# Two attention stages: loops unrolled, four slots of q and K, K loaded once per head group, value products two key tiles at a time

## The chip, the cores and the metric

The kernel runs on one core of a Trainium2 chip. Its engines are TensorE (PE; a weight load, PEld, goes ahead of each matmul), VectorE (DVE), ScalarE (ACT), GpSimd (POOL) and SyncE (SP), which issues the DMAs. Each runs its own list of instructions in order and waits on semaphores for the others. The metric is the time of one execution in microseconds (us), the median of several runs; lower is better.

## The reference

Four blocks on x (1024 tokens by 512), each followed by a residual sum and a layer norm: a causal self-attention with an adapter, a lookup block, a second causal self-attention, and a gated feed-forward block. The change touches the inside of the two attentions:

```python
# layer 0: 32 heads of 16 for q, k and v; layer 1: 32 heads of q, 8 of k and v (4 q heads share one)
scores = einsum("bhqd,bhkd->bhqk", q, k) / sqrt(16)      # q, k after rotary embedding
scores = where(causal, scores, -inf)
attn = softmax(scores, axis=-1)                          # T = 1024 tokens
y = einsum("bhqk,bhkd->bhqd", attn, v)
```

## The kernel before

An attention is done in 8 **head groups** g of R = 4 heads. A group has two **units**, c = 0 (queries 0 to 511, 4 key tiles of 128) and c = 1 (queries 512 to 1023, 8 key tiles), because of the causal mask. For each unit:

- **Maxima** (`entry`, L841 to L868). The row maxima of the scores are found ahead: PE multiplies a query tile (96 rows: q and k are cut into bf16 parts that are stacked) with `k_max` into one of three PSUM banks (`RING`), adds a mask on the diagonal (L866), and DVE takes the maximum into `mx` (L1035). One such piece is an *entry*: 12 entries for c0, 28 for c1. After the last one DVE joins the halves (L1042, c1 only) and cuts the maxima into three bf16 parts in four dependent operations on 16 columns (L1046 to L1053). One more entry, "T", is PE's transpose of these parts (L850); DVE copies it to `mT` (L1024), and SP copies `mT` in three DMAs (`load_max`, L805) into rows 96 to 98 of the stacked q. The maxima of group g+1 are done while group g is in its scores and values; entries are dealt out evenly over the *slots* between them (`slot`, L918).
- **Scores** (L883): `k_exp` (96 rows and 3 rows of -1) times the stacked q with its maxima, 99 rows deep, so that the product comes shifted by its maximum. Two heads are a *pair* n; pairs use two PSUM pairs in turn, so pair n waits for exp n-2 (L879).
- **Exp** (L980) on ACT, into one of `NP_RING` = 4 buffers of `arena_p`.
- **Masking** (L1098): POOL zeroes what lies above the diagonal in the last four key tiles of a unit with `affine_select`.
- **Values** (L903): four matmuls in float32 of 32 columns each, side by side in the array, per key tile; then ACT copies the sum to `o_raw` (L987). POOL copies the v of a group to `v_grp` (L1078).

In the loop (`step`, L923 to L937) each key tile has: scores of the next tile (pair, slot, pair, slot), slot, values of this tile, slot. Two groups are one turn of a hardware loop (`Fori`), so that DMA addresses come from registers.

SP loads from DRAM what `load_and_project` stored there: q of a unit (3 DMAs, 2 slots per c), and K of a group twice, as `k_max` and as `k_exp` (3 DMAs each, 2 slots each; the rows of one part are read for 3, 2 and 1 stacked parts: `broadcast_to`, L711). `k_max` of group g+2 is loaded into the slot of group g once the maxima of g+1 that stand ahead are done. SP's list is in order: `mT`, q, `k_exp`, `mT`, q, `k_max`. In layer 1 K has 1 head for a group, not 4. `load_first` is issued earlier, for layer 0 in the adapter stage, for layer 1 between the stores of the projection (L362).

Of the kernel before, what the change touches and what calls it, by code (L numbers as in the profile page):

```python
# [32 lines left out]
P = 128  # L33
# [5 lines left out]
R = 4  # L39
# [16 lines left out]
NP_RING = 4  # L56
# [49 lines left out]
def build(nc, d, out):  # L106
    with ExitStack() as stack:
# [13 lines left out]

        arena_s = at("arena_s", M_S, [P, 12288])
# [74 lines left out]
        attention(nc, 0, att, stacked, arena_o, arena_p, v_tok, v_grp, ident_b, maskb, psum)  # L197
# [15 lines left out]
        attention(nc, 1, att, stacked, arena_o, arena_p, v_tok, v_grp, ident_b, maskb, psum)  # L213
# [468 lines left out]
class StackedOperands:  # L682


    def __init__(self, ph, layer, arena_s, q_parts, k_parts):
        self.q_parts, self.k_parts = q_parts, k_parts
        self.kr = R if layer == 0 else 1
        self.q = view(arena_s, 0, [2, CH, R * 512], BF16)
        self.k_max = view(arena_s, 16384, [2, R * T], BF16)
        self.k_exp = view(arena_s, 32768, [2, R * T], BF16)  # L690
        self.q_loaded = [[ph.sem(f"q_loaded{s}{c}") for c in range(CH)] for s in range(2)]
        self.km_loaded = [ph.sem(f"km_loaded{s}") for s in range(2)]
        self.ke_loaded = [ph.sem(f"ke_loaded{s}") for s in range(2)]
# [6 lines left out]
    def load_q(self, sp, g, s, c):  # L700

        for j0, n in ((0, 3), (3, 2), (5, 1)):
            sp.dma_start(
                self.q[D * j0:D * (j0 + n), s, c, :].rearrange("p (h t) -> p h t", h=R),
                self.q_parts[bass.ds(R * g, R), 0:n, :, 512 * c:512 * c + 512]
                .rearrange("h j d t -> j d h t")).then_inc(self.q_loaded[s][c], 16)

    def load_k(self, sp, g, s, dst, sem):

        for kp, (j0, n) in enumerate(((0, 3), (3, 2), (5, 1))):  # L710
            sp.dma_start(  # L711
                dst[D * j0:D * (j0 + n), s, 0:self.kr * T],
                self.k_parts[kp, :, bass.ds(self.kr * g, self.kr), :]
                .rearrange("(o d) h t -> o d (h t)", o=1).broadcast_to([n, D, self.kr * T]))\
                .then_inc(sem[s], 16)

    def load_first(self, queue):

        self.load_q(queue, 0, 0, 0)
        self.load_k(queue, 0, 0, self.k_max, self.km_loaded)  # L720


def attention(nc, layer, phase, stacked, arena_o, arena_p, v_tok, v_grp, ident_b, maskb, psum):
# [4 lines left out]


    kr, q_st, k_max, k_exp = stacked.kr, stacked.q, stacked.k_max, stacked.k_exp  # L730
    q_loaded, km_loaded, ke_loaded = stacked.q_loaded, stacked.km_loaded, stacked.ke_loaded
# [1136 lines left out]
```

## Time and profile before

| | |
|---|---|
| time, median of 3 runs (lowest, highest) | 1092.92 us (1092.42 to 1098.62) |
| profiled execution: its span | 1084.4 us |
| what lies around the span (median less span) | 8.5 us |
| TensorE busy | 924.4 us, 85% |
| VectorE busy | 700.9 us, 65% |
| ScalarE busy | 485.7 us, 45% |
| GpSimd busy | 254.2 us, 23% |
| mean granted clock of TensorE | 0.917 |
| attention stages | about 150 to 471 us (layer 0) and 635 to 900 us (layer 1) |

Busy time is the sum over the instructions of an engine. The granted clock is the share of its full rate that TensorE was allowed; it is 1.0 (2.4 GHz) or 0.5 (1.2 GHz) at any one time. The span is from the first to the last instruction of the profiled execution.

### The profile page before, as it was taken

What the parts mean: (1) busy time and instruction counts of PE and PEld (TensorE: products, weight loads), DVE (VectorE), ACT (ScalarE), POOL (GpSimd) and SP (SyncE); (2) the same over time, 40 slices, a digit from 0 to 9 for tenths busy, and PEclk for the clock granted to TensorE, in tenths of its full rate; (3) what the DMA queues carried; (4) which work ended last, traced back from release to release, by engine and by line L of the source; (5) the groups of instructions that cost most, each with busy time, mean ns of one, the idle gap of its engine ahead of it and who ended that gap; (6) DMA issues with size and microseconds to landing.
All of it is one profiled execution on the core that took longest, in us unless ns stands there. A gap on an engine that the chain in (4) does not pass through costs nothing. (4 is left out here: it accounts for less than half of the span.)

```text
span 1084.4 us, 17334 instructions
## 1 busy us (share of the span) xinstructions
PE 924.4 (85%) x5462; PEld 512.0 (47%) x5462; DVE 700.9 (65%) x1305; ACT 485.7 (45%) x750; POOL 254.2 (23%) x397
## 2 busy tenths in 40 slices
PE   7879943789988898888977877999999988799998
PEld 5557821333333333257535532333444426677766
DVE  6975332668666766448584765988888835745564
ACT  4221401336544655642262213566666673346730
POOL 2554020022112111210614531221212223012300
PEclk9998965889889989999788977999999999999999
DMA  9221161112211321020001330011111101042001
GB/s 315 88 89 59 23 144 42 42 48 87 71 56 59 81 72 54 11 97 1 1 0 56 103 94 23 24 46 46 46 44 44 24 1 39 11 173 78 20 21 59
DMA packets 45537, 64.87 MB, mean 60 GB/s; under 512 B 9056, under 2 KB 32160, under 8 KB 43936
## 3 DMA queue, kind: packets, MB, share of 16 engines
q1 hardware_dynamic: 45472, 64.01, 19.7%
q8 instruction: 40, 0.66, 0.3%
q14 instruction: 25, 0.20, 0.1%
HBM read 51.27 MB, written 12.32 MB: 59 GB/s over the span
## 5 line engine op out<-in xcount | busy, mean ns | idle before, releaser
L1035 DVE TENSOR_REDUCE mx<-psum 128x1 f32<-128x512 f32 (+3 forms) x640 | 372.1, 632 | 157.9 <-PE psum L866 132.1
L980 ACT ACTIVATE arena_p<-psum 128x1024 f32<-128x1024 f32 (+3 forms) x384 | 294.0, 808 | 271.5 <-PE psum L883 270.7
L861 PE MATMUL psum<-arena_s 96*128 96x512 bf16 (+3 forms) x768 | 236.7, 349 | 53.8 <-DMA arena_s<-k_parts 43.4
L883 PE MATMUL psum<-arena_s 99*128 99x512 bf16 (+3 forms) x768 | 191.1, 340 | 30.3 <-DMA arena_s<-mT 26.7
L1098 POOL TENSOR_SCALAR_AFFINE_SELECT arena_p<-arena_p 128x256 f32<-128x256 f32 x256 | 102.8, 407 | 472.5 <-ACT arena_p L980 470.7
L903 PE MATMUL psum<-arena_p,v_grp 128*32 128x512 f32 (+3 forms) x1536 | 171.2, 519 | 2.1 <-POOL arena_p L1098 1.9
L861 PEld LDWEIGHTS psum<-arena_s 96*128 96x128 bf16 x768 | 77.5, 102 | 200.9 <-DVE mx L1035 107.4
L883 PEld LDWEIGHTS psum<-arena_s 99*128 99x128 bf16 x768 | 64.9, 100 | 94.9 <-ACT arena_p L980 23.4
L866 PE MATMUL psum<-maskb,ident_b 128*128 128x128 bf16 x512 | 109.1, 235 | 0.0
L255 PE MATMUL psum<-x_h,w 128*128 128x512 f32 x224 | 89.9, 465 | 10.4 <-DVE w L472 7.3
L866 PEld LDWEIGHTS psum<-maskb,ident_b 128*128 128x128 bf16 x512 | 54.1, 106 | 13.0 <-issue 1.6
L255 PEld LDWEIGHTS psum<-x_h,w 128*128 128x128 f32 x224 | 46.0, 205 | 27.7 <-issue 9.3
L903 PEld LDWEIGHTS psum<-arena_p,v_grp 128*32 128x32 f32 x1536 | 30.8, 110 | 52.9 <-issue 40.7
L430 ACT CAST arena_p<-arena_o 128x512 bf16<-128x512 f32 x26 | 16.1, 619 | 86.2 <-DMA q_parts<-arena_p 41.1
L1654 PE MATMUL psum<-x_h,ff_w 128*128 128x512 f32 (+1 forms) x176 | 45.7, 403 | 1.7 <-ACT ff_flags L1711 0.9
L255 PE MATMUL psum<-x_l,w 128*128 128x512 f32 x112 | 47.0, 419 | 0.0
L464 DVE CAST arena_p<-arena_o 128x512 bf16<-128x512 f32 x26 | 32.3, 1241 | 20.6 <-POOL arena_o L538 20.4
L1654 PE MATMUL psum<-x_l,ff_w 128*128 128x512 f32 (+1 forms) x176 | 45.5, 401 | 0.0
L1191 PE MATMUL psum<-wo_h,yT 128*128 128x512 f32 x128 | 43.8, 403 | 1.6 <-DVE arena_s L1264 1.6
L1674 PE MATMUL psum<-ff_wd,ff_g 128*128 128x512 f32 (+1 forms) x176 | 41.5, 396 | 1.6 <-ACT ff_wd L1707 1.6
L538 POOL TENSOR_TENSOR arena_o<-arena_o,arena_p 128x512 f32<-128x512 f32 x26 | 31.8, 1225 | 45.3 <-ACT arena_p L430 45.3
L534 POOL TENSOR_TENSOR arena_o<-arena_o 128x512 f32<-128x512 f32 x26 | 34.2, 1317 | 31.6 <-DVE arena_o L490 31.5
(200 smaller groups left out, 1087.3 us busy)
## 6 DMA issues: line engine op xcount, KB each, us to landing
q_parts<-arena_p SPq DMA_DIRECT2D x48, 128.0 KB
arena_s<-q_parts SPq DMA_DIRECT2D x32, 192.0 KB, 3.0
arena_s<-k_parts SPq DMA_DIRECT2D x16, 384.0 KB
ff_raw<-in_w_in SPq DMA_DIRECT2D x11, 512.0 KB, 3.5
arena_s<-q_parts SPq DMA_DIRECT2D x32, 128.0 KB, 2.9
arena_s<-k_parts SPq DMA_DIRECT2D x16, 256.0 KB
k_parts<-arena_p SPq DMA_DIRECT2D x30, 128.0 KB
arena_w<-in_w SPq DMA_DIRECT2D x12, 256.0 KB, 6.5
```

The costliest lines, as they stand in the source:

```text
L255: last = pe.matmul(out, lhs[i](k), rhs[j](k), start=k + n == 0, stop=k == KC - 1 and n == 2)
L534: pool.tensor_tensor(rotated(n), t_cos[:, s, :], t_sin[:, s, :], ALU.add)\
L861: last = pe.matmul(psum[:, bank, width * n:width * n + width], q_st[0:KS, s, c, 512 * r + P * i:512 * r + P * i + P], k_max[0:KS, s, T * k ...
L866: last = pe.matmul(psum[:, bank, width * (n + 1) - P:width * (n + 1)], ident_b[:, :], maskb[:, :], start=False, stop=True)
L883: last = pe.matmul(psum[:, 2 * hp + h, o:512], k_exp[0:KM, s, T * kh + P * kt:T * kh + P * kt + P], q_st[0:KM, s, c, 512 * r + o:512 * r + ...
L903: last = pe.matmul(psum[32 * r:32 * r + VW, 6, o:512], v_grp[:, s, kt, r if layer == 0 else 0, :], pr[:, (n + r // 2) % NP_RING, r % 2, o: ...
L980: act.activation(pr[:, n % NP_RING, :, o:512], psum[:, 2 * (b % 2):2 * (b % 2) + 2, o:512], ACT.Exp, scale=scale).then_inc(exp_ready, 1)
L1035: dve.tensor_reduce(mx[:, kc, col:col + 4 * len(heads) - 3:4], src, AX, ALU.max)\
L1098: pool.affine_select(out=tri, in_=tri, compare_op=ALU.is_ge, fill=0.0, base=0, pattern=[[0, 2], [1, P]], channel_multiplier=-1).then_inc(m ...
L1191: last = pe.matmul(psum[:, 5, :], yT_hl[i][:, t % 2, k, :], w_out[j][:, k, :], start=k + n == 0, stop=k == KC - 1 and n == 2)
L1654: last = pe.matmul(psum[0:rows[i], 2 * (n % 3) + u, :], ff.w_hl[a][:, i % 2, col:col + rows[i]], x_hl[b][:, k, 512 * c:512 * c + 512], sta ...
L1674: return pe.matmul(psum[:, 4 + t % 2, :], ff.g_hl[a][0:rows[i], i, P * t:P * t + P], ff.wd_hl[b][0:rows[i], i, :], start=(a, b, i) == (0, ...
```

## The change

It touches `StackedOperands`, `attention` and two constants, for both layers:

- The `Fori` loops are gone: all engines' lists are written out for 16 units u = 2g + c, with constant addresses and semaphore values.
- K has one array `k_st` with 4 slots by group, used for maxima and scores alike, loaded once (`load_k`); q has 4 slots by unit, loaded four units ahead. `load_first` loads q of four units and K of two groups; the attention's own list starts with K of groups 2 and 3.
- `mT` goes into the stacked q in one DMA instead of three.
- The maxima's cutting into parts moves from DVE (4 operations) to POOL (`split_max`); DVE keeps the join (`join_max`), which comes after the first entry of the list of the next unit.
- T stands at place 4 of a list (counted from 0) instead of place 2. All entries of units 0 and 1 come ahead of the first scores; then the list of unit u+2 is dealt out over unit u, as before.
- Scores are two key tiles ahead; the value products of two key tiles come near each other.
- `NP_RING` = 8; `arena_x` (the place of `xT`, not in use in the attention) holds the other half.
- v is copied by unit; `copy_o` of unit u-1 comes after the exp number 3 of unit u.

```diff
-NP_RING = 4
+NP_RING = 8
+NS = 4
@@ StackedOperands
-        self.q = view(arena_s, 0, [2, CH, R * 512], BF16)
-        self.k_max = view(arena_s, 16384, [2, R * T], BF16)
-        self.k_exp = view(arena_s, 32768, [2, R * T], BF16)
+        self.q = view(arena_s, 0, [NS, R * 512], BF16)
+        self.k = view(arena_s, 16384, [NS, self.kr * T], BF16)
+    def load_first(self, sp):
+        for u in range(NS):
+            self.load_q(sp, u)
+            if u % CH == 0:
+                self.load_k(sp, u // CH)
@@ attention
+    TURN_AT = 4
+    def entries(b):
+        out = pieces(b) if b < NU else []
+        if b >= 1:
+            out.insert(min(TURN_AT, len(out)), "T")
+        return out
@@ sync
+            def load_max(u):
+                s = u % NS
+                sp.wait_ge(qk_taken, turn_entry(u) + 1)
+                sp.dma_start(q_st[KS:KM, s, :].rearrange("j (a q) -> j a q", q=P), mT[:, u % 2, :])\
+                    .then_inc(max_loaded[s], 16)
...
+            for g in range(CH, NS):
+                stacked.load_k(sp, g)
+            load_max(0)
+            for u in range(NU):
+                if u + 1 < NU:
+                    load_max(u + 1)
+                if u + NS < NU:
+                    sp.wait_ge(scores_ready, first_exp[u + 1])
+                    stacked.load_q(sp, u + NS)
+                g, c = divmod(u, CH)
+                if c == 1 and g + NS < NG:
+                    sp.wait_ge(scores_ready, first_exp[u + 1])
+                    stacked.load_k(sp, g + NS)
@@ tensor
+            for b in range(2):
+                for n, what in enumerate(lists[b]):
+                    entry(first_entry[b] + n, b, what)
+            for u, kt in blocks[0:2]:
+                for p in range(2):
+                    scores(u, kt, p)
+            for u, (c, _) in enumerate(steps):
+                todo = lists[u + 2] if u + 2 <= NU else []
+                n_slots = 4 * n_tiles[c]
...
+                def maxima(slot):
+                    nonlocal issued
+                    while issued < (len(todo) if u + 2 == NU else len(todo) * slot // n_slots):
+                        entry(first_entry[u + 2] + issued, u + 2, todo[issued])
+                        issued += 1
...
+                at = blocks.index((u, 0))
+                for n in range(0, n_tiles[c], 2):
+                    ahead = blocks[at + n + 2:at + n + 4]
+                    for k, (au, akt) in enumerate(ahead):
+                        for p in range(2 - k):
+                            scores(au, akt, p)
+                            maxima(4 * n + 2 * k + p + 1)
+                    values(u, n)
+                    maxima(4 * n + 5)
+                    values(u, n + 1)
+                    maxima(4 * n + 7)
+                    if ahead:
+                        scores(*ahead[1], 1)
+                    maxima(4 * n + 8)
@@ scalar
+            for u in range(NU):
+                for b in range(2 * n_tiles[steps[u][0]]):
+                    exp(u, b)
+                    if u and b == 3:
+                        copy_o(u - 1)
+            copy_o(NU - 1)
@@ vector
+            for b in range(NU + 1):
+                if b == NU:
+                    join_max(b - 1)
+                for n, what in enumerate(lists[b]):
+                    if n == 1 and b and steps[b - 1][0] == 1:
+                        join_max(b - 1)
@@ gpsimd
+            def load_v(u):
+                n = n_tiles[steps[u][0]]
+                g = steps[u][1]
+                if u >= 2:
+                    pool.wait_ge(pv_done, first_exp[u - 1])
+                pool.tensor_copy(v_grp[:, u % 2, 0:n, 0:kr, 0:D], ...)
...
+            def split_max(u):
+                s, c = u % 2, steps[u][0]
+                m, (high, mid, low) = mx[:, s, 0, :], [mst[:, s, j, :] for j in range(NPART)]
+                if c == 1:
+                    pool.wait_ge(max_joined, u // CH + 1)
+                else:
+                    pool.wait_ge(qk_taken, first_entry[u] + len(lists[u]))
+                if u >= 2:
+                    pool.wait_ge(qk_ready, turn_entry(u - 2) + 1)
+                pool.tensor_copy(high, m).then_inc(max_high, 1)
+                pool.wait_ge(max_high, u + 1)
+                pool.tensor_tensor(md[:, :], m, high, ALU.subtract).then_inc(max_rest, 1)
+                pool.wait_ge(max_rest, u + 1)
+                pool.tensor_copy(mid, md[:, :]).then_inc(max_mid, 1)
+                pool.wait_ge(max_mid, u + 1)
+                pool.tensor_tensor(low, md[:, :], mid, ALU.subtract).then_inc(max_ready, 1)
...
+            for u in range(2):
+                load_v(u)
+            for u in range(2):
+                split_max(u)
+            for u, (c, g) in enumerate(steps):
+                for b in range(8 * c, 8 * c + 8):
+                    n = first_exp[u] + b
+                    o = first_column(c, b // 2)
+                    pool.wait_ge(exp_ready, n + 1)
+                    tri = pr[n % NP_RING][:, :, o:o + P]
+                    pool.affine_select(out=tri, in_=tri, ...).then_inc(masked, 1)
+                if u + 2 < NU:
+                    split_max(u + 2)
+                    load_v(u + 2)
```

## Rows read from the trace of the kernel before

**Rows 1.** Busy time of each engine in stretches: span, length, busy (instructions), clock, DMA

```profile
290.00:330.00 40.00, 34.71 (x256) 14.28 (x248) 28.23 (x56) 22.02 (x30) 7.38 (x18) 0.91 0.28 73
750.00:790.00 40.00, 39.41 (x313) 16.66 (x310) 34.71 (x68) 25.36 (x36) 10.26 (x26) 1.00 0.12 32
```

**Rows 2.** Timeline, ACT: start, us, engine, line, operation; both layers

```profile
283.03 0.59 ACT L987 COPY arena_o<-psum 128x512 f32 x1
...
426.56 0.59 ACT L987 COPY arena_o<-psum 128x512 f32<-128x512 f32 x1
...
768.84 0.59 ACT L987 COPY arena_o<-psum 128x512 f32 x1
...
798.28 0.59 ACT L987 COPY arena_o<-psum 128x512 f32 x1
```

**Rows 3.** Timeline, PE, layer 0; in brackets the idle time before and its end

```profile
309.25 0.26 PE L861 MATMUL psum<-arena_s 96*128 96x128 bf16 x1 [5.29 <-DMA arena_s<-k_parts]
```

**Rows 4.** Timeline, SP, layer 0

```profile
280.54 2.33 SPq L711 DMA_DIRECT2D arena_s<-k_parts  x3
286.39 1.84 SPq L808 DMA_DIRECT2D arena_s<-mT  x3
...
290.07 3.21 SPq L711 DMA_DIRECT2D arena_s<-k_parts  x3
```

**Rows 5.** Busy time by stretch, layer 0; last: clock, DMA share, GB/s

```profile
298.00:303.00 5.00, 5.00 (x45) 1.98 (x38) 4.49 (x8) 2.66 (x5) 1.94 (x5) 1.00 0.14 58
```

**Rows 6.** One line's instructions (L808), 286 to 288.4 us

```profile
DMA to landing us min/median/max: 2.2/2.2/10.9
```

**Rows 7.** Timeline, PE, layer 1

```profile
776.87 0.60 PE L883 MATMUL psum<-arena_s 99*128 99x512 bf16 x2
...
781.36 1.06 PE L903 MATMUL psum<-arena_p,v_grp 128*32 128x512 f32 x8
782.35 0.34 PE L861 MATMUL psum<-arena_s 96*128 96x384 bf16 x1
```

**Rows 8.** Timeline, ACT, layer 1

```profile
777.51 1.94 ACT L980 ACTIVATE arena_p<-psum 128x1024 f32<-128x1024 f32 x2 [0.68 <-PE psum L883]
```

**Rows 9.** Timeline, all engines, layer 1, end of a unit c1

```profile
788.30 0.43 PE L903 MATMUL psum<-arena_p,v_grp 128*32 128x128 f32 x8
...
788.66 0.39 PE L861 MATMUL psum<-arena_s 96*128 96x512 bf16 x1
...
790.16 0.17 DVE L1042 TENSOR_TENSOR mx<-mx 128x16 f32<-128x16 f32 x1
...
791.12 0.17 DVE L1053 TENSOR_TENSOR mst<-md,mst 128x16 bf16<-128x16 f32 x1
```

**Rows 10.** Groups by shape, POOL, layers 0 and 1: busy, mean ns | idle before

```profile
L1098 POOL TENSOR_SCALAR_AFFINE_SELECT arena_p<-arena_p 128x256 f32<-128x256 f32 x256 | 102.8, 407 | 472.5 <-ACT arena_p L980 470.7
...
L1078 POOL COPY v_grp<-v_tok 128x512 f32 x6 | 3.7, 609 | 0.0
...
L1078 POOL COPY v_grp<-v_tok 128x128 f32 x6 | 1.7, 289 | 0.0
```

**Rows 11.** Timeline, POOL, start of the kernel

```profile
2.48 0.29 POOL L521 TENSOR_SCALAR_AFFINE_SELECT maskb<-maskb 128x128 bf16<-128x128 bf16 x1 [0.23 <-POOL ident_b L519]
```

**Rows 12.** Timeline, PE, layer 1, first units

```profile
667.10 0.22 PE L850 MATMUL psum<-ident_b,mst 128*48 128x128 bf16 x1 [0.97 <-DVE mst L1053]
671.00 1.46 PE L883 MATMUL psum<-arena_s 99*128 99x512 bf16 x3 [3.69 <-DMA arena_s<-mT]
```

**Rows 13.** Busy time by stretch, just after Rows 12

```profile
671.00:678.00 7.00, 7.00 (x37) 2.76 (x38) 1.85 (x3) 4.45 (x5) 0.00 (x0) 0.61 0.31 84
```

**Rows 14.** Timeline, PE, layer 0, the first scores

```profile
182.06 1.86 PE L883 MATMUL psum<-arena_s 99*128 99x512 bf16 x4 [16.40 <-DMA arena_s<-mT]
```

**Rows 15.** Timeline, SP, projection of layer 1

```profile
619.99 1.35 SPq L703 DMA_DIRECT2D arena_s<-q_parts  x3
...
623.48 10.96 SPq L359 DMA_DIRECT2D q_parts<-arena_p  x9
```

More of the change, by code:

```diff
@@ L717, in load_first @@
[L717 to L731, printed above, removed]
+                .then_inc(self.k_loaded[g % NS], 16)
+    def load_first(self, sp):
[3 more added lines that the diff above has]
+                self.load_k(sp, u // CH)
@@ L776, in attention @@
-        RING = (4, 5, 7)
-        first0 = len(entries(0, with_t=False))
-        start = first0 + len(entries(1))
-        n_entries = [len(entries(c)) for c in range(CH)]
-        EG = sum(n_entries)
-        assert EG % len(RING) == 0
-        def first_entry(g, c):
-            at = start + (n_entries[0] if c else 0)
-            return EG * g + at, at
-        def first_column(c, kt):
-            return max(0, P * kt - 512 * c)
-        def pairs(engine, body, first=None):
-            if first:
-                first()
-            with engine.Fori(1 if first else 0, NG // 2 - 1) as pair:
-                body(pair, False)
-            body(NG // 2 - 1, True)
@@ L873, in scores @@
                 o = first_column(c, kt)
[L874 to L886 removed]
+                if kt == 0 and p == 0:
+                    pe.wait_ge(max_loaded[u % NS], 16 * (u // NS + 1))
+                    if u == 0:
+                        pe.wait_ge(rows, NS)
@@ L887, in scores, with values @@
+                if n >= 2:
+                    pe.wait_ge(exp_ready, n - 1)
+                for t in range(2):
+                    r = 2 * p + t
+                    at = T * key_head(r) + P * kt
+                    last = pe.matmul(psum[:, 2 * (n % 2) + t, o:512], k_st[0:KM, g % NS, at:at + P],
+                                     q_st[0:KM, u % NS, 512 * r + o:512 * r + 512], start=True, stop=True)
                 last.then_inc(scores_ready, 1)
-            def values(pair, s, c, kt):
-                g = 2 * pair + s
-                n = first_half[c] + 2 * kt
+            def values(u, kt):
+                c = steps[u][0]
+                n = first_exp[u] + 2 * kt
@@ L939, in listed @@
-            def listed(number, at, todo, pair, s, c):
-                return [(number + n, at + n, what, pair, s, c, n == 0) for n, what in enumerate(todo)]
-            def body(pair, last):
-                for a in range(2):
-                    alone = last and a == 1
-                    nxt = (pair, 1) if a == 0 else (pair + 1, 0)
-                    for c in range(CH):
-                        todo = listed(*first_entry(2 * pair + a, c),
-                                      entries(c, not alone, not (alone and c == 1)), *nxt, c)
-                        step(pair, a, c, alone, todo, 1 if alone else 4 * n_tiles[c])
@@ L1056, in _ @@
-            unit(0, 0, entries(0, with_t=False), 0, 0)
-            unit(first0, first0, entries(1), 0, 1)
-            def body(pair, last):
-                for a in range(2):
-                    alone = last and a == 1
-                    for c in range(CH):
-                        if not (alone and c == 1):
-                            unit(*first_entry(2 * pair + a, c), entries(c, not alone),
-                                 2 * pair + a + 1, c)
-            pairs(dve, body)
         @block.gpsimd
```

337 lines of the change are left out of this document (107 added, 230 removed).

## The prediction

> **What bounds the kernel now.** I read the granted clock and busy times by stretch first, then the waits of the two attention stages, then the order of instructions around each. All edits lie in the attentions, 150 to 471 us (layer 0) and 635 to 900 us (layer 1). TensorE (PE) is the bound in both, but not equally well used: in 40 us of layer 1 it is busy for 39.4 at clock 1.00, in 40 us of layer 0 for 34.7 at 0.91 [rows 1]. One head group (units c0 and c1) takes 768.84 to 798.28 = 29.4 us in layer 1, but 283.03 to 426.56, four groups, in layer 0, 35.9 each [rows 2]. The difference is one wait per group of layer 0: the maxima of the next group wait 5.3 us for `k_max` [rows 3]; each such wait is followed by a stretch at half clock. VectorE (DVE) is second, 34.7 of 40 us in layer 1 [rows 1].
>
> Why K is late: its loads start at 280.54 (`k_exp`) and 290.07 (`k_max`) [rows 4], and 8 us after the second the 16 DMA engines are busy to a share of 0.14 only, at 58 GB/s [rows 5]. The K copies (a broadcast of 3, 2 and 1 rows of 16 by 8 KB) are thus done by about two engines, for some 15 us each. Copies issued behind them are late too: of the three `mT` copies issued at 286.39 [rows 4], two land after 2.2 us and one after 10.9 [rows 6], which is 16.8 after K's first issue.
>
> **The change part by part.**
>
> *K once, four slots, static addresses.* The 5.3 us wait goes: K of group g+4 is issued two whole groups before its maxima need it. This and the half-clock stretch behind it give layer 0 back what it lost against layer 1: 35.9 - 29.4 = 6.5 us a group. In layer 1 PE never waits for K: no gain. Unrolled loops: PE's timeline shows no idle time at the seams, so 0.
>
> *Values in runs of two.* One block of four heads takes 781.36 to 782.35 = 0.99 us for 512 columns [rows 7], one of 128 takes 788.30 to 788.66 = 0.36 [rows 9], so 0.15 doesn't grow with the columns, and some 0.1 is lost ahead of it. The new code puts `maxima(4n + 5)` between the two `values`, and the lists (29 entries in 32 slots, 13 in 16) have one or two entries there. So the run is broken except in the last two units; I take 0. Had it held, six changes of kind fewer a group gave 6 x 0.25 = 1.5 us, 18 in all.
>
> *The scores are bunched.* Score pairs share two PSUM pairs, so pair n waits for exp n-2. Before, a value block lies in each period. Now the order is S(3,1), S(4,0), S(4,1), S(5,0), with one entry between each. From the start of a pair [rows 7] to its exp are 776.87 to 777.51 = 0.64 us, exps follow each other in 1.94 / 2 = 0.97 [rows 8], so S(5,0) can't start before 0.64 + 1.94 + 0.1 = 2.7 us after S(3,1); PE has three pairs (1.3) and three entries (0.75) to fill them: 0.6 us lost. In the first such period of c1 the copy of `o_raw` (0.59) stands between the two exps: 1.2. Narrower tiles lose less, and where DVE is late they lose nothing. For c1 that is between 0.6 and 2.2; I take 1.5 us a group.
>
> *The split of the maxima goes to GpSimd (POOL).* DVE loses five operations on 16 columns for c1, 790.16 to 791.29 = 1.1 us, and four for c0 [rows 9], and gets one join back. PE waited 0.97 us for this chain ahead of one T [rows 12], shorter elsewhere; I take -0.7 a group. But POOL works in order, and between the selects of unit u and those of unit u+1 now stand split_max(u+2) and load_v(u+2). For u+2 = c1 the split waits for join_max, which DVE does after the first entry of the *next* list, in unit u+1 = c0, whose first value block needs selects standing behind it. The path, from PE's last list entry of unit u (788.66 in the trace of before): DVE is through with its queue 1.5 us later [rows 9]; first entry of the next list and join 0.6; four dependent operations of POOL. None of 16 columns stands in the trace: a copy of 128 is 0.29, of 512 0.61 [rows 10], so some 0.2 for 16, and a wait for POOL's own last operation is 0.23 [rows 11]. 4 x 0.2 + 3 x 0.23 = 1.5 (1.1 to 1.9). Then load_v 0.29 (layer 1) or 0.61 (layer 0), two selects of 0.41 with their waits 0.9 [rows 10], handover 0.1. Together 4.9 and 5.2 us. PE reaches the block after about 1.6 us of pairs and entries. Stall: 3.3 us in layer 1, 3.6 in layer 0, every group (2.8 to 3.8).
>
> *The transpose of the maxima, T.* At place 4 of 13 entries it falls to slot 7 of the short unit, right behind the second value block; then come one narrow pair, one entry, and S of unit u+2, which needs the `mT` copy. The same sequence at its tightest is in the trace: T at 667.10, next scores at 671.00, 3.7 us idle [rows 12]. There the last of three copies counted, issued 1.2 us behind the first; now it is one. 3.7 - 1.2 - 0.4 (pair and entry) = 2.1 us a group in layer 1 (1.7 to 3.3). In layer 0 the copy stands behind K of group g+4, issued at the end of unit u, some 12 us ahead of it; K lands 13 to 17 us after its issue ([rows 3, 4, 6]: 17 with others in the way), and PE's stall is 2.1 to 4.9 us; I take 3.7, nearer to the row of 16.8. The Trainium skill, "DMA: Bandwidth & Descriptors", section "Why a DMA increments its semaphore by 16 and not by 1", says that a copy uses the largest number of engines up to 16 that divides the slowest dimension of both sides, the lowest-numbered ones. By it K's copies are on 3, 2 and 16 engines, as the low share agrees, and the new one-piece `mT` copy (3 rows out of 48) is on the same lowest three, so it can't pass K. Were it not behind K, layer 0 would have layer 1's 2.1, and the sum 6 x 1.6 = 10 us less.
>
> *Clock.* After the 3.7 us stall the next 7 us are granted 0.61 [rows 13]: 2.7 us of work lost. For layer 0 I keep the present 1.7 us a group of half clock, of which the fixed landing of `mT` swallows 1.0. For layer 1, whose stalls are shorter than that one, I take none; with one in each group it is up to 16 us more.
>
> *Ends.* First unit: all 40 entries of units 0 and 1 now run ahead of the first scores, but DVE has the same work by the end of unit 1; layer 0 has `mT` behind four K loads instead of three (it was 182.06, after a wait of 16.4 [rows 14]), yet more of the maxima done by then: -4. In layer 1 the early loads put 12 more DMAs among the stores of the projection, which keep SyncE issuing until the attention starts (the last nine take 10.96; three loads of q 1.35, so 0.45 each [rows 15]): 12 x 0.45 = +5; 0 if the stores wait for other things. Last units: no maxima are left to fill the exp periods, and the POOL stall stays: +4 a layer.
>
> **Sum.** Layer 1: 29.4 - 0.7 + 1.5 + 3.3 + 2.1 = 35.6, +6.2 a group. Layer 0: 29.4 - 0.7 + 1.5 + 3.6 + 3.7 + 0.7 = 38.2, +2.3 on 35.9. Six full groups each: 37 + 14 = 51; starts +1, ends +8: +60. The profiled span of 1084.4 becomes 1144.4; the median of the runs, 1092.9, lies 8.5 above the span, so 1153 us. What hides this edit's other work (four memsets of POOL, 12 more loads of q ahead): the 30 us ahead of the first scores in layer 0; uncovered it is 7 us of memset.
>
> **The rivals.**
> *The intended effect*: the new waits are covered and only the K wait counts. For it: POOL's chain is my estimate alone, DVE has 1.9 us a group less. Against: the order of POOL's program is plain, and it must pass before a value block. It gives layer 0 6.5 + 0.7 and layer 1 0.7 a group: 6 x 7.9 = 47 less, ends the same: about 1045. It decides if the POOL path is under 1.6 us; chance 0.13.
> *A draw*: join and selects come early enough to halve both stalls (2.7 and 3.6 a group less), and the bunching costs nothing (1.5): 4.2 and 5.1 less, 60 - 6 x 9.3 = +4: 1097. Chance 0.09.
> *Each group of layer 1 drops to half clock too*, or the upper ends hold for POOL and bunching as well: +16 to +32: 1169 to 1185. For it: [rows 12, 13]; against: 3.3 us stalls are shorter and work lies between the two. Chance 0.2.
> *The run of two holds, as it says*: 18 us less than forecast, 1135; within my case. That the unrolled code is fetched too late I give no case of its own: the straight-line stages show PE over 0.9 busy.
> The forecast's own case, 1110 to 1168, has 0.56; some 0.02 lies above 1190.
>
> **How the numbers follow.** A measurement of this kernel tells about 1% (11 us) from no change. Faster by over 1%: the intended effect and the low edge of the draw, 0.14. Within 1%: the draw's rest, 0.08. Slower: 0.78. The range takes in forecast, draw and clock case, 1090 to 1190; 0.14 + 0.04 lie outside.
>
> **What the profile after would show.** No wait of `mx` products for `k_parts` in the middle of layer 0. In each c0 unit PE idle for 3 us ahead of the first value block (named POOL select), with POOL's four 16-column operations and the v copy just ahead of its select, and 2 us ahead of S for `mT`, longer in layer 0. Idle ahead of S for exps in c1. Copies of `o_raw` 35 to 36 us apart in layer 1, 38 in layer 0. The prediction is wrong if POOL's split ends before PE needs the select, if PE runs list entries in place of waiting (its order forbids it), or if the `mT` copy overtakes K.

## The result, and the profile after

| | before | after |
|---|---|---|
| median (lowest to highest) | 1094.91 us (1092.42 to 1098.62) | 1218.99 us (1218.21 to 1230.77) |
| ratio, 95% interval | | 1.117 (1.111 to 1.123) |
| span | 1084.4 us | 1217.8 us |
| mean granted clock | 0.917 | 0.868 |
| TensorE busy | 924.4 us, 85% | 993.2 us, 82% |

The change makes the kernel 124 us slower: the sign was forecast, and the size is outside the forecast's range of 1090 to 1190 us. The median of before is of four runs here, of three in the table further up. The two spans differ by 133 us and the medians by 124, because the 8.5 us by which the median of before lay above its span is mostly no fixed part: a run's time is at most some 2 us above its own span wherever both are on record (1219.56 and 1217.8 us for the kernel after), so the profiled execution of before was one of some 1086 us, faster than the median. The mean clock says how long TensorE was at half rate: twice what is missing from 1. That is 2 x 0.083 x 1084.4 = 180 us before and 2 x 0.132 x 1217.8 = 321 us after. The clock row of the page after, in 40 slices of the span:

```profile
PEclk9989855888988888898789659889898888989999
```

Counted from 0, the attentions are slices 5 to 17 and 22 to 34. Each starts with two slices at 5 to 6 tenths and stays at 8 or 9 tenths behind them. Next, busy time by stretch: span, length, busy time and instructions of PE, PEld, DVE, ACT and POOL, then clock, DMA share and GB/s. The first two rows are six head groups of layer 0 and of layer 1:

```profile
242.50:497.60 255.10, 204.66 (x1356) 73.10 (x1356) 146.63 (x259) 113.92 (x157) 51.99 (x156) 0.88 0.11 28
764.50:1007.10 242.60, 205.39 (x1356) 72.68 (x1356) 146.62 (x259) 113.93 (x158) 49.13 (x156) 0.87 0.08 20
902.70:925.10 22.40, 20.62 (x145) 7.09 (x145) 16.74 (x29) 12.77 (x19) 4.21 (x13) 1.00 0.08 20
924.50:928.50 4.00, 1.49 (x16) 0.84 (x14) 2.29 (x6) 2.44 (x5) 1.79 (x8) 1.00 0.00 0
930.00:934.00 4.00, 3.11 (x18) 0.92 (x15) 2.10 (x4) 0.38 (x1) 0.69 (x2) 0.50 0.00 0
934.00:938.00 4.00, 3.15 (x10) 1.25 (x10) 0.93 (x2) 1.82 (x2) 0.00 (x0) 0.50 0.37 103
```

A group takes 255.1 / 6 = 42.5 us in layer 0 and 242.6 / 6 = 40.4 in layer 1, against 35.9 and 29.4 [rows 2]. Layer 1, which nothing held up before (clock 1.00 in [rows 1]), is the one to read. The copies of `o_raw` in the ACT timeline mark its units:

```profile
902.67 0.58 ACT L935 COPY arena_o<-psum 128x512 f32<-128x512 f32 x1
...
925.09 0.58 ACT L935 COPY arena_o<-psum 128x512 f32<-128x512 f32 x1
...
942.83 0.58 ACT L935 COPY arena_o<-psum 128x512 f32<-128x512 f32 x1
```

The long unit c1 took 22.4 us at full clock (20.1 before), the short unit c0 17.7 (9.3 before). So 8.4 of the 10.7 us lie in c0. Its PE timeline, with the idle time ahead of an instruction and what ended it in brackets:

```profile
926.23 0.28 PE L863 MATMUL psum<-arena_s 99*128 99x128 bf16 x2 [0.35 <-ACT arena_x L927]
...
928.55 1.06 PE L881 MATMUL psum<-arena_p,v_grp 128*32 128x512 f32 x8 [1.80 <-POOL arena_p L1021]
...
930.62 1.51 PE L881 MATMUL psum<-arena_p,v_grp 128*32 128x384 f32 x8
932.06 0.30 PE L828 MATMUL psum<-ident_b,mst 128*48 128x128 bf16 x1
...
934.85 1.03 PE L863 MATMUL psum<-arena_s 99*128 99x512 bf16 x2 [1.74 <-DMA arena_s<-mT]
```

These are the two waits that the prediction names, in their places: the first value block waits for POOL's select, the first scores of the next unit, a c1, for the `mT` copy. Between them the clock falls to half. The same value block takes 1.06 us at 928.55 and a narrower one 1.51 at 930.62, and the rows above show 0.50 up to 938. What POOL did just ahead of the select:

```profile
926.49 0.20 POOL L999 CAST mst<-mx 128x16 bf16<-128x16 f32 x1 [6.24 <-DVE mx L949]
926.77 0.22 POOL L1001 TENSOR_TENSOR md<-mx,mst 128x16 f32<-128x16 f32 x1
927.05 0.20 POOL L1003 CAST mst<-md 128x16 bf16<-128x16 f32 x1
927.32 0.22 POOL L1005 TENSOR_TENSOR mst<-md,mst 128x16 bf16<-128x16 f32 x1
927.48 0.29 POOL L985 COPY v_grp<-v_tok 128x128 f32<-128x128 f32 x1
927.73 1.48 POOL L1021 TENSOR_SCALAR_AFFINE_SELECT arena_p<-arena_p 128x256 f32<-128x256 f32 x4
```

POOL was idle for 6.24 us until DVE's join. The exps that these four selects follow were done by 925.20, so the selects waited for the split and the copy alone. PE's waits, summed over the kernel (us in total, times, longest):

```profile
PE psum L863 <- DMA arena_s<-mT: 54.1, 15, 16.7
PE psum L881 <- POOL arena_p L1021: 27.3, 15, 2.1
PE psum L863 <- ACT arena_p L927: 22.3, 67, 0.7
PE psum L863 <- ACT arena_x L927: 16.3, 40, 0.8
...
PE psum L841 <- DMA arena_s<-k_parts: 12.4, 1, 12.4
```

The maxima wait for K once only, at the start; the wait of [rows 3] is gone, as meant. In layer 0 it came back under another name, on the scores:

```profile
299.57 1.03 PE L863 MATMUL psum<-arena_s 99*128 99x512 bf16 x2 [6.29 <-DMA arena_s<-mT]
```

### The profile page after: what moved, and what is told of

Its sections match the earlier page's. It is cut to its first block and busy times, and to the rows that moved or that the text cites. A ratio compares the mean times of both kernels' runs of the same rounds, so it can differ in the third digit from the quotient of the medians.

```text
span 1217.8 us, 14933 instructions
## 1 busy us (share of the span) xinstructions
PE 993.2 (82%) x5462; PEld 511.4 (42%) x5462; DVE 684.9 (56%) x1177; ACT 482.3 (40%) x750; POOL 283.4 (23%) x545
## 5 line engine op out<-in xcount | busy, mean ns | idle before, releaser
L863 PE MATMUL psum<-arena_s 99*128 99x512 bf16 (+3 forms) x768 | 210.6, 362 | 96.7 <-DMA arena_s<-mT 54.1
L927 ACT ACTIVATE arena_p<-psum 128x1024 f32<-128x1024 f32 x192 | 175.1, 954 | 238.0 <-PE psum L863 237.7
L841 PE MATMUL psum<-arena_s 96*128 96x512 bf16 (+3 forms) x768 | 253.0, 372 | 17.2 <-DMA arena_s<-k_parts 12.4
L927 ACT ACTIVATE arena_x<-psum 128x512 f32<-128x512 f32 (+1 forms) x192 | 120.8, 676 | 177.1 <-PE psum L863 177.0
L863 PEld LDWEIGHTS psum<-arena_s 99*128 99x128 bf16 x768 | 57.1, 103 | 198.1 <-ACT arena_p L927 67.0
L881 PE MATMUL psum<-arena_p,v_grp 128*32 128x512 f32 (+1 forms) x768 | 111.9, 666 | 27.3 <-POOL arena_p L1021 27.3
L845 PE MATMUL psum<-maskb,ident_b 128*128 128x128 bf16 x512 | 118.1, 249 | 0.0
L1021 POOL TENSOR_SCALAR_AFFINE_SELECT arena_p<-arena_p 128x256 f32<-128x256 f32 x128 | 49.7, 406 | 168.1 <-ACT arena_p L927 168.1
L881 PE MATMUL psum<-arena_x,v_grp 128*32 128x256 f32 (+2 forms) x768 | 73.5, 462 | 0.8 <-POOL arena_x L1021 0.8
L1021 POOL TENSOR_SCALAR_AFFINE_SELECT arena_x<-arena_x 128x256 f32<-128x256 f32 x128 | 49.7, 406 | 91.4 <-ACT arena_x L927 72.2
```

The source lines that it names most:

```text
L841: last = pe.matmul(psum[:, bank, width * n:end], q_st[0:KS, b % NS, 512 * r + P * i:512 * r + P * i + P], k_st[0:KS, g % NS, at:at + width ...
L845: last = pe.matmul(psum[:, bank, end - P:end], ident_b[:, :], maskb[:, :], start=False, stop=True)
L863: last = pe.matmul(psum[:, 2 * (n % 2) + t, o:512], k_st[0:KM, g % NS, at:at + P], q_st[0:KM, u % NS, 512 * r + o:512 * r + 512], start=Tr ...
L881: last = pe.matmul(psum[32 * r:32 * r + VW, 6, o:512], v_grp[:, u % 2, kt, r if layer == 0 else 0, :], pr[(n + r // 2) % NP_RING][:, r % 2 ...
L927: act.activation(pr[n % NP_RING][:, :, o:512], psum[:, 2 * (n % 2):2 * (n % 2) + 2, o:512], ACT.Exp, scale=scale).then_inc(exp_ready, 1)
L1021: pool.affine_select(out=tri, in_=tri, compare_op=ALU.is_ge, fill=0.0, base=0, pattern=[[0, 2], [1, P]], channel_multiplier=-1).then_inc(m ...
```

## The experiments

The theory after the result (A in most runs): two idle stretches of under 2 us in each c0 unit cost more by the half clock that follows than by themselves (experiment 4 prices both: about as much); the rest is the bunched order of scores, and, in layer 0, K's loads ahead of `mT`. The rivals (B) have the loss in another part or in the waits alone. Ratios are to the kernel before, measured beside each; "less" and "faster" are between medians. A group is a c0 and a c1.

**1. POOL's split and v copy moved ahead of the selects that wait long anyway** (c1), and behind the first four in c0:

```diff
                 for b in range(8 * c, 8 * c + 8):
+                    if b == (8 * c if c or u == NU - 2 else 4) and u + 1 < NU:
+                        split_max(u + 1)
+                        load_v(u + 1)
...
-                if u + 2 < NU:
-                    split_max(u + 2)
-                    load_v(u + 2)
```

> The changed kernel (1219 us) with one edit: in a c0 unit GpSimd masks its first four tiles' halves before it splits the next maxima. Theory A (each c0 unit has two stalls of some 2 us, and the two together pull TensorE's clock to half for about 10 us, which costs more than the stalls): the 1.8 to 2.1 us wait for GpSimd ahead of the first value block goes, the wait for mT stays, half-clock time falls by a third or more; 14 units x (2 + 2) = 56 us less, about 1160 us. Rival B (the half clock comes from the thin TensorE work between the scores, whatever the stalls): only the stall goes, 14 x 2 = 28 us less, 1190 us, half-clock time unchanged.

1182.59 us, ratio 1.081 (1.074 to 1.088): 36 us less. The select's wait is gone from PE's list, that for `mT` stays. Six groups of layer 1, by stretch:

```profile
754.00:973.00 219.00, 190.92 (x1356) 69.14 (x1356) 146.39 (x259) 113.25 (x158) 49.06 (x153) 0.95 0.09 22
```

That is 36.5 us a group, so 3.9 less for a wait of 1.8; the clock in the stretch rose from 0.87 to 0.95. In layer 1 the wait cost twice its length, as A has it. The whole is nearer to B's 1190 than to A's 1160, and that is layer 0's part: there PE now stands 7.6 to 8.5 us for `mT` in the four groups with K loads in flight (3.1 to 6.3 before this edit), and a group is only 1.5 us shorter.

**2. The order of scores and values of before**, one key tile ahead:

```diff
-            for u, kt in blocks[0:2]:
+            for u, kt in blocks[0:1]:
...
+                for kt in range(n_tiles[c]):
+                    ahead = blocks[at + kt + 1:at + kt + 2]
+                    for p in range(2):
+                        if ahead:
+                            scores(*ahead[0], p)
+                        maxima(4 * kt + p + 1)
+                    maxima(4 * kt + 3)
+                    values(u, kt)
+                    maxima(4 * kt + 4)
```

> The changed kernel with the order of scores and values of the kernel before (scores one key tile ahead, one value block a tile). Theory A: the mT wait of c0 units goes in layer 1 (1.75 us) and most of it in layer 0, the exp waits go (c1 unit from 22.4 to about 20.2 us), the wait for GpSimd stays, and with one stall left the half-clock time falls; 12 x (2.2 + 2 + 2) + what layer 0 waits more, some 85 us less, about 1130 us. Rival B: bunching is a matter of the exp waits alone, 12 x 2.2 = 27 us less, 1190 us, and the mT wait moves but stays.

1160.25 us, ratio 1.062 (1.054 to 1.070): 59 us less, for an order that the prediction had priced at 1.5 us a group:

```profile
732.90:939.80 206.90, 179.00 (x1349) 72.61 (x1349) 142.08 (x258) 115.95 (x158) 51.66 (x163) 0.97 0.09 24
```

34.5 us a group, 5.9 less than the change, with POOL's wait still there (14.6 us in these six groups) and the `mT` wait gone from them. The time is midway between A and B; one more wait, for `copy_o`, came in (10.4 us in these groups) and is the subject of the next run.

**3. Both.**

> The changed kernel with both edits of the two runs above. Theory A: all new waits but layer 0's first mT wait go; layer 1 runs a group in 29 us as before or less, and layer 0 too, since K comes once and early: before's 1094 less 6 x 6.5 us of the K wait, plus 8 us of the projection's longer end and 10 us of the start of layer 0: about 1073 us. Rival B (VectorE or the single list order leaves another 2 us a group): about 1100 us. Rival C (the layer 0 mT copies still wait behind K): layer 0 at 33 us a group, about 1095 us.

1138.70 us, ratio 1.040 (1.032 to 1.047). This is slower than all three cases. In layer 1 a group takes 34.0 us, still 4.6 above before, at a clock of 0.95 in the first four of them:

```profile
728.80:762.90 34.10, 30.80 (x226) 12.25 (x226) 24.03 (x44) 19.32 (x28) 8.45 (x26) 0.95 0.12 31
```

PE now waits for something that it never waited for in the change, and did in experiment 2 (30.1 us):

```profile
PE psum L881 <- ACT arena_o L931: 45.7, 29, 1.8
```

With one key tile ahead, value block 0 of a unit comes before exp 3, but `copy_o` of the unit before, which must empty its PSUM bank, stands behind exp 3. So `copy_o`'s place and the new order belong together.

**4. Work added.** In each c0 unit 8 matmuls of 512 columns (k by k, into a free bank, read by nobody) ahead of the first value block, and 8 ahead of the first scores of the next unit:

```diff
...
                         for p in range(2 - k):
+                            if c == 0 and n == 2 and k == 0 and p == 0 and u + 2 < NU:
+                                fill(8)
...
+                    if c == 0 and n == 0 and u + 2 < NU:
+                        fill(8)
                     values(u, n)
```

> The changed kernel with eight more matmuls of 512 columns (1.7 us at full clock) put into a free PSUM bank ahead of each of the two waits of a c0 unit; their results are overwritten and not used. It tells whether it is the idle time that pulls the clock down. Theory A (idle TensorE pulls the clock down): the half-clock stretches of layer 1's middle go or shrink to a third, and though work is added, which fills the stalls, the time falls by 6 to 12 units x 3 to 4 us: about 1180 us. Rival B (the clock falls for another reason): the fill runs in the stalls, the time stays at 1219 us or rises by up to 20 us, and half-clock time is unchanged.

1187.51 us, ratio 1.085 (1.079 to 1.092): 224 matmuls more, and 31 us faster than the change. By stretch, and the fill in PE's timeline:

```profile
749.50:972.20 222.70, 203.25 (x1452) 75.99 (x1452) 145.76 (x259) 112.91 (x158) 49.12 (x156) 1.00 0.09 22
```

```profile
751.03 1.89 PE L910 MATMUL psum<-arena_s 96*128 96x512 bf16 x8
753.00 1.06 PE L881 MATMUL psum<-arena_p,v_grp 128*32 128x512 f32 x8
...
756.07 1.89 PE L910 MATMUL psum<-arena_s 96*128 96x512 bf16 x8
758.32 0.61 PE L863 MATMUL psum<-arena_s 99*128 99x512 bf16 x2 [0.35 <-DMA arena_s<-mT]
```

Each fill of 1.89 us takes the place of an idle stretch; the value block starts no earlier after the last scores, but the clock is 1.00. A group takes 222.7 / 6 = 37.1 instead of 40.4: 3.3 us of each group of layer 1 were half clock and nothing else, beside 1.80 + 1.74 = 3.5 us of standing still: about as much, not more. This is the run that separates the waits' length from their effect on the clock. In layer 0, where the `mT` waits outlast the fill (up to 4.7 us) and the clock is 0.96, a group gained 1.4 us. A holds.

**5. Experiment 3 with `copy_o` after exp 1** (`if u and b == 1:`).

> The changed kernel with the GpSimd order and the score order of e3, and ScalarE's copy of the finished unit's sum after the next unit's exp 1, not 3, as in the kernel before. In e3 TensorE waited 45.7 us in 29 value blocks for this copy. Theory A (that wait, with the clock it costs, is what layer 1 has left over the kernel before): layer 1's groups from 34.0 to 29.4 us, layer 0 by 2 to 5 us each, together 40 to 55 us less than e3's 1139: about 1090 us. Rival B (taken away, another wait of the same instruction comes up, mT or the mask): no more than 15 us less, 1125 us.

1090.22 us, ratio 0.997 (0.995 to 0.999). Layer 1 takes 29.1 us a group, as before the change, and waits neither for `mT` nor, but for 0.2 us in all, for POOL's selects. Layer 0's first four groups with K loads in flight don't follow; their stretch, and the kernel's `mT` waits:

```profile
228.80:392.40 163.60, 126.71 (x906) 50.63 (x904) 96.03 (x173) 77.61 (x105) 35.27 (x104) 0.87 0.18 40
```

```profile
PE psum L863 <- DMA arena_s<-mT: 52.3, 5, 16.0
```

40.9 us a group, against 29.1 for the same program text after the last K load. A holds, in size and in place.

**6. The change with K loaded by six copies of 16 rows**, in place of three that broadcast one source to 3, 2 and 1 parts:

```diff
-        for kp, (j0, n) in enumerate(((0, 3), (3, 2), (5, 1))):
...
-                self.k[D * j0:D * (j0 + n), g % NS, :],
-                .rearrange("(o d) h t -> o d (h t)", o=1).broadcast_to([n, D, self.kr * T]))\
-                .then_inc(self.k_loaded[g % NS], 16)
+        for j, kp in enumerate((0, 0, 0, 1, 1, 2)):
...
+                self.k[D * j:D * (j + 1), g % NS, :],
+                .rearrange("d h t -> d (h t)")).then_inc(self.k_loaded[g % NS], 16)
...
-                        pe.wait_ge(k_loaded[g % NS], 48 * (g // NS + 1))
+                        pe.wait_ge(k_loaded[g % NS], 96 * (g // NS + 1))
```

> The changed kernel (1219 us) with K loaded in six copies of 16 rows from 16 rows, in place of three that read 16 rows for 48, 32 and 16; nothing else. Theory A (the three copies keep two or three DMA engines for 15 us, and mT and its like queue behind them): layer 0's groups fall from 42 to 44 us to layer 1's 40 or a little over, its mT waits from 3 to 6 us to 1.8, and the first scores of layer 0 come some 15 to 25 us earlier; 6 x 3 + 20 = 38 us less, about 1180 us; layer 1 unchanged. Rival B (the DMA engines share their time among what is queued, so mT doesn't wait for K): only the start is earlier, 1200 us.

1188.94 us, ratio 1.085 (1.080 to 1.090): 30 us less. First the copies of one K load in the middle of layer 0 (L712), then PE's `mT` waits:

```profile
DMA to landing us min/median/max: 3.6/4.6/5.2
```

```profile
PE psum L862 <- DMA arena_s<-mT: 26.3, 14, 2.1
```

Longest 2.1 us, also in layer 0 and at the start of it; there the second copy of `o_raw` came 20.5 us earlier (222.06 against 242.55). A group of layer 0 now takes 40.9 us on average, 1.6 less, as in layer 1, which did not change (40.8). So most of the 2.1 us by which a group of layer 0 was longer were K ahead of `mT`, and the 20.5 us of the start as well. B, by which `mT` doesn't wait for K, is false: the longest `mT` wait fell from 16.7 to 2.1 us.

**7. Experiments 5 and 6 together.**

> e5 and e6 together: all four edits to the changed kernel. Theory A: both layers run a group in 29 to 30 us, layer 0 without waits for K or mT; 1094 less 45 us for the K wait of the kernel before, less some 10 for its start, plus 8 for the longer projection: about 1045 us. Rival B (a limit of its own in layer 0, such as the larger K rows): layer 0 stays at 33 us or more a group, 1075 us.

1018.13 us, ratio 0.930 (0.926 to 0.935). Six groups of layer 1:

```profile
632.40:807.30 174.90, 173.94 (x1359) 71.79 (x1357) 143.57 (x259) 115.15 (x158) 49.83 (x155) 1.00 0.12 29
```

PE is busy for 173.9 of 174.9 us, and both layers take 29.1 us a group. A's time was 27 us too long. The unrolled lists cost nothing that shows here.

**8. The kernel before with K in six copies**, nothing of the change:

> The kernel before (1094 us) with both its K loads in six copies of 16 rows, nothing else. Theory A (it was the layout of the copies and not their number or date that made K late): the seven waits of 4.7 to 5.7 us go and with them the half clock, layer 0's groups from 35.9 to 29.6 us, the start of layer 0 some 10 to 20 us shorter: 55 us less, about 1040 us. Rival B (the wait is for the place of the load in SyncE's list and 12 more DMA issues a group make it later still): no gain or a loss, 1095 us or more.

1026.37 us, ratio 0.937 (0.932 to 0.941). This one edit gives 66 us (A had 55; B is false), and the wait of [rows 3] is gone with two K loads a group kept. The stretches behind a K issue at 246.71:

```profile
246.00:248.00 2.00, 1.43 (x9) 0.66 (x8) 1.03 (x3) 0.61 (x1) 0.63 (x2) 1.00 0.95 234
...
252.00:254.00 2.00, 2.00 (x18) 0.83 (x16) 1.94 (x5) 1.61 (x2) 0.00 (x0) 1.00 0.22 31
```

The share is about full for 6 us and then back to 0.22. In the kernel before, the four us behind the K issue of 290.07 [rows 4] look like this, and 8 us behind it there were still 0.14 and 58 GB/s [rows 5]:

```profile
290.00:294.00 4.00, 4.00 (x31) 1.41 (x24) 3.27 (x5) 2.95 (x4) 0.61 (x2) 1.00 0.66 129
```

The Trainium skill, "DMA: Bandwidth & Descriptors", section "Why a DMA increments its semaphore by 16 and not by 1", has a copy on the largest number of engines, up to 16, that divides the slowest dimension of both sides. By that rule a leading 3 or 2 of the broadcast held the copy to 3 or 2 engines, and 16 rows are spread over all 16. These runs agree with it: a short full share with six copies, a long low tail with three, and the landing within 5.2 us.

**9. Experiment 7, and in layer 1 only q and K of unit 0 are loaded among the stores of the projection**, the rest at the head of the attention's list.

> e7 (1018 us) with one more edit: in layer 1 only q and K of the first unit are loaded among the projection's stores, the other three units of q and K of group 1 after them. Theory A (the 12 added issues hold up the stores, so that layer 1's attention starts some 8 us later than it could): 5 to 8 us less, 1011 us. Rival B (ScalarE's wait of 10.6 us ahead of the v transposes has another cause): within 3 us of e7.

1011.76 us, ratio 0.926 (0.923 to 0.929), the fastest kernel of the study, 6.4 us below experiment 7. Its first copy of `o_raw` in layer 1 is at 603.21, against 612.13 there. A holds.

**10. The change with `copy_o` after exp 1 alone.**

> The changed kernel (1219 us) with ScalarE's copy after exp 1 of the next unit, nothing else. It tells how much of the 2.3 us by which a c1 unit grew is this copy between two exps that the bunched scores wait for. Theory A (it is half of it): c1 units from 22.4 to 21.3 us, 14 x 1.1 = 15 us less, 1204 us. Rival B (the exps alone): unchanged, 1219 us, and then the v copy or the exps end the same wait.

1226.53 us, ratio 1.121 (1.116 to 1.125), no faster than the change. A forecast 1204 us and is false: c1 takes 22.6 us and more. But the edit moves the copy and doesn't take it away, and the ACT copy now waits for value products:

```profile
806.00 0.58 ACT L935 COPY arena_o<-psum 128x512 f32<-128x512 f32 x1 [1.44 <-PE psum L881]
```

What the copy costs where the change has it can be read from the trace after: in the c1 of 902.7 to 925.1 PE stands 0.58 us for the exp behind the copy (904.23) and 0.23 us at the same place of the next bunch (909.64). So the copy is some 0.35 of the 2.3 us by which c1 grew; the rest are the exps.

**11. Experiment 9, but with the change's own order of scores and place of `copy_o`**: POOL's order and the loads are mended, the bunching is not.

> e9 with the changed kernel's own order of scores and values and its place of ScalarE's copy (so: the change with GpSimd's order, K's copies and the early loads mended). It prices the score order alone. Theory A (the order costs the exp waits of c1, the mT wait of c0 and, through the second, the clock): c1 units 22.4, c0 units 11 to 15 us, 12 x (2.2 + 4) = 75 us more than e9, about 1085 us. Rival B (with one stall a group left the clock stays up): c0 11 us, 12 x 4.3 = 50 us more, 1060 us. Rival C (the order is free once the stalls are gone): as e9.

1127.86 us, ratio 1.030 (1.026 to 1.034): the order with its copy alone costs 116 us against experiment 9, which is 43 us more than A and more than all cases. Six groups of layer 1, and PE's waits:

```profile
695.20:916.90 221.70, 193.54 (x1356) 69.79 (x1356) 146.55 (x259) 113.48 (x158) 49.23 (x153) 0.94 0.09 22
```

```profile
PE psum L866 <- DMA arena_s<-mT: 29.3, 14, 2.2
PE psum L866 <- ACT arena_p L930: 22.0, 68, 0.7
PE psum L866 <- ACT arena_x L930: 16.9, 41, 0.8
```

36.95 us a group against 29.1. Once K is out of the way, the `mT` wait exists in this order only: experiments 7 and 9 show none above 0.2 us, with the same single copy and the same place of T. Not every such wait brings the clock down. It was 2.1 to 2.2 us in all six c0 units of this stretch; five ran at a clock of 0.78 to 0.88 and took 14.1 to 15.4 us, and one kept 1.00 and took 12.8:

```profile
806.30:821.50 15.20, 12.41 (x81) 4.84 (x81) 7.69 (x16) 6.19 (x11) 2.96 (x10) 0.78 0.10 27
843.90:856.70 12.80, 9.73 (x81) 4.14 (x81) 7.51 (x16) 6.00 (x10) 2.96 (x10) 1.00 0.11 32
```

**12. Experiment 11 with the fill of 8 matmuls ahead of the `mT` wait**:

> e11 (1128 us) with eight added matmuls (1.7 us at full clock) in a free PSUM bank ahead of the mT wait of each c0 unit, results not used. It tells what of the score order's price is waiting and what is the clock it drags down. Theory A (the mT wait still pulls the clock to half): granted clock of layer 1's middle 1.00, groups from 36.9 to some 34.5 us, 12 x 2.4 = 29 us less, 1099 us. Rival B (the clock is down there for the exp waits of the bunched pairs, or it costs nothing): 1128 us or more.

1102.26 us, ratio 1.009 (1.005 to 1.013): 26 us faster with 112 matmuls more, as A has it.

```profile
656.90:868.40 211.50, 192.46 (x1404) 71.71 (x1404) 145.71 (x259) 112.84 (x158) 50.27 (x156) 1.00 0.10 26
```

35.25 us a group at clock 1.00. So a single idle stretch of about 2 us a group costs 1.7 us of half clock on top of itself, on average over the groups. The many waits for exps, 0.7 us at most, left the clock at 1.00. The run also prices the rest of the order: c1 22.4 and c0 12.8 us, against 20.2 and 8.9 in experiment 9, of which about 2 in c0 is the wait that the fill covers.

## Why the prediction was right about the sign and wrong about the size

The span grew by 133 us where +60 was forecast. In the median it is 124 for 60: the forecast median of 1153 us counted the 8.5 us above the span as fixed, which they are not. One group of layer 1, term by term:

| term | forecast | measured | from |
|---|---|---|---|
| POOL's select | +3.3 | +1.8 | PE's waits after |
| wait for `mT` | +2.1 | +1.7 to 2.1 | PE's waits after |
| half clock behind the stalls | 0 | +3.3 | experiment 4 |
| bunching less the shorter chain | +0.8 | about +4 | c1 and c0 of experiments 9 and 12 |
| group | 35.6 | 40.4 | |

**The step that failed** is the one on the clock: "For layer 1, whose stalls are shorter than that one, I take none; with one in each group it is up to 16 us more". The rival built on it had a chance of 0.2 and a price of 16 us. The reason given, that [rows 12, 13] have a single stall of 3.7 us and these are shorter, doesn't hold: 1.80 and 1.74 us, with 4.5 us of work between them, took the clock down in each of the six c0 units (to 0.64 to 0.89 on average), and experiments 11 and 12 show it for one such stall in five units of six. In layer 1 this was 6 x 3.3 = 20 us. For layer 0 no run prices the kept 1.7 by itself. The other large miss, the bunching, has the same size (3.2 us a group).

**The bunching was mis-sized.** I priced it for c1 only and took back 0.7 for the shorter chain of the maxima. Measured are 22.4 - 20.2 = 2.2 in c1 (my upper bound) and about 1.7 in c0. Of the 0.7 at most 0.3 came back: experiment 9 takes 29.1 us a group for the 29.4 of before. The copy of `o_raw` between the exps, for which I took 0.6, is some 0.35 (experiment 10). The order also brings the `mT` wait with it. The place of T, with few entries and one narrow pair behind it, is the cause I gave; with scores one key tile ahead the next unit's scores come a tile later behind the same T, and experiment 7 shows no wait.

**POOL** was right in mechanism and place, and too dear. Four operations took 926.49 to 927.54 = 1.05 us for a forecast of 1.5, since they start 0.28 us apart and the wait for the own last one is some 0.08, not the 0.23 of [rows 11]. DVE was no earlier: from PE's last list entry (924.19) to the join (926.25) are 2.1 us, as forecast. From that entry to the value block are 4.4 us instead of 4.9, and PE gets there 2.6 us behind it instead of 1.6, since it stands 0.40 and 0.35 us for exps on the way; this overlap of two terms was not in the sum. The stall is 1.8 instead of 3.3, but by experiment 1 its removal gave 3.9 a group, so the sum of stall and clock was near the term by luck.

**K ahead of `mT`** was right: the maxima's wait went, the `mT` copy didn't pass K, and PE stood up to 6.29 us. The term of 3.7 fits the mean of six waits (3.75) by luck: it was meant for every group, but K loads are in flight in four of them only, with waits of 5.10, 6.29, 3.11 and 4.21 (4.7 on average), and the other two have 1.85 and 1.94. A group of layer 0 came to 42.5 against 38.2; with K out of the way it runs as in layer 1 (experiment 6), so what it has above the forecast beside K are the same clock and bunching. The cause lay one level deeper than the order of the queue: the K copies themselves (experiment 8). The prediction had read the low share and used it only as a reason why `mT` can't pass.

**Ends.** The first unit of layer 0 was forecast at -4. From the first maxima to the second copy it took 91.9 us instead of 80.3, +11.6:

```profile
158.00:182.00 24.00, 6.05 (x21) 2.13 (x21) 7.28 (x17) 0.00 (x0) 0.00 (x0) 0.50 0.16 62
```

```profile
158.00:180.00 22.00, 14.36 (x47) 4.18 (x47) 15.88 (x29) 0.00 (x0) 7.35 (x8) 0.51 0.25 76
```

The first row is of the kernel before, the second of the one after: both do these maxima at half clock, the change only does more of them. What set the start was `mT`. First SP's list of before, then that of after, and PE after:

```profile
153.64 11.60 SPq L711 DMA_DIRECT2D arena_s<-k_parts  x3
165.29 1.86 SPq L808 DMA_DIRECT2D arena_s<-mT  x3
```

```profile
149.76 20.83 SPq L712 DMA_DIRECT2D arena_s<-k_parts  x6
170.64 0.77 SPq L799 DMA_DIRECT2D arena_s<-mT  x1
```

```profile
195.91 1.89 PE L863 MATMUL psum<-arena_s 99*128 99x512 bf16 x4 [16.73 <-DMA arena_s<-mT]
```

The `mT` copy was issued 5.3 us later, behind one more K load, and the scores that wait for it began 25.3 us behind its issue instead of 16.8 [rows 14]. So they began 13.9 us later, and the maxima done early gave back some 2.5 of it up to the second copy. Experiment 6 took 20.5 us off this start. The four memsets of POOL (13.9 us in the trace after, two with 7.0 before) are hidden here, as the prediction had it; with K out of the way (experiment 7) they are not, and PE stands 7.0 us for POOL ahead of the first T. Layer 1's loads among the stores cost 8 us up to the attention, for +5; experiment 9's first copy of layer 1 came 8.9 us earlier by moving them, its median 6.4. The first unit of layer 1 took 4 us more, for which the sum has no term. The last groups took +3 a layer for the forecast 4. The runs of two value tiles are broken up as forecast: the blocks at 928.55 and 930.62 have four entries between them.

The terms close: layer 1's groups are 6 x 4.8 = 29 above forecast, layer 0's 6 x 4.3 = 26, starts and ends 29 for 9 and so 20; less 2, since layer 1's six groups of before take 29.7 us each and not the 29.4 of the one in [rows 2]. Together that is the 73 us missed.

What stays open: why a stall of 2.1 us takes the clock down in five c0 units and not in the sixth; and how the 3.3 us of half clock divide between the two stalls of a c0 unit, for the runs that cover one alone (experiments 1 and 12) start from different kernels.

## What to carry to other kernels

A regular idle stretch of TensorE of about 2 us cost its length and then about as much again by the half clock behind it, in this kernel: price it at twice, and test it by filling the hole with idle matmuls, which tells the two apart in one run. A small, late copy was here only as early as the big ones ahead of it, and a low DMA share beside a long landing was the sign that the big ones used few engines: look at their shape before their order (experiment 8 gave 66 us by the shape alone). When an order of scores, exps and values is changed, the small steps tied to it (the copy that frees a bank, the place of a transpose) must be placed anew with it.

## What the runs showed that I had not expected

- Two stalls of 1.80 and 1.74 us, 4.5 us apart, gave a granted clock of 0.50 from 930 to 938 us, after 1.00 in all of the unit before. 16 added matmuls in a c0 unit, 1.89 us for each 8, made the kernel 31 us faster.
- A K load in six copies of 16 rows, issued with nothing large ahead of it, landed within 5.2 us of its issue (experiment 6) and showed a DMA share of 0.95 at 234 GB/s (experiment 8); as three broadcast copies it showed 0.66 at 129 GB/s in the first four us and still 0.14 at 58 GB/s 8 us behind its issue. In the kernel before this was worth 66 us, more than the 47 us that the prediction gave the change at its best.
- POOL does four dependent operations on 128x16 in 1.05 us (0.20 and 0.22 us each, 0.27 to 0.28 from start to start).
